# Copies of h, a power and the dense sums taken earlier, weight halves spread over ScalarE's waits, in a one-core attention and mixture-of-experts kernel

## The chip, the cores and the metric

The kernel runs on one core of one Trainium2 chip. The metric is device microseconds of one execution. The core has TensorE (PE in the rows, its weight loads PEld), VectorE (DVE), ScalarE (ACT), GpSimd (POOL) and the queue of SyncE (SP), which issues the transfers.

## The reference

```python
x = x + tanh(g_xattn) * attention(layernorm(x), ctx, ...)   # 8 batches x 128 tokens x 512, 32 heads, 8 kv heads
h = layernorm(x)                                            # seen by the router as 4 batches of 256 tokens
ratio = mean(|h[vision:]|) / (mean(|h[:vision]|) + 1e-8)    # one number for each batch
scores = softmax(concat(h, ratio) @ gate_w + gate_b)        # 3 experts
top_val, top_idx = top_k(scores, 2); top_val /= sum(top_val) + 1e-8
# an expert is chosen for each slot from the FIRST token: j = top_idx[:, 0, i]
pre = h @ w1[e] + b1[e]; act = (tanh, gelu, silu)[e](pre); out_e = act @ w2[e] + b2[e]
x = x + tanh(g_ffn) * (top_val[0] * out_of_slot_0 + top_val[1] * out_of_slot_1)
```

All arithmetic is float32. In the kernel a product of two float32 matrices is three products of rounded halves (hi x hi, lo x hi, hi x lo).

## The kernel before

The order of the work on each engine is written out by hand. Engines meet only in semaphores, and each engine takes its own instructions strictly in the order of the code.

The attention goes through 64 units (8 groups of heads x 8 batches) in a software pipeline, and ends in a drain. During and after the drain the second layer begins. Its steps, for batch b:

- `norm_row(1, b)` (ACT) writes the normalised row of h into `rows`. It needs the mean and the deviation: `h_stats(b)` (DVE), `h_pow(b)` (POOL, L1239), `h_neg_mean(b)` (DVE, L1467).
- `h_transpose(b)` (PE, L509) turns it into PSUM. From b = 4 on it waits for `h_lo_(b - 2)`, which frees the bank.
- `h_hi_(b)` (ACT, L1038) copies the rounded half into `xT_hi`, `h_lo_(b)` (DVE, L1280) the rest into `xT_lo`.
- `sum_abs(b)` (ACT, L1033) sums |h| for the ratio.

Six dense tiles follow on PE, `dense(l)` (L288, 12 matmuls each, into two PSUM banks in turn), for batches 0 and 1 and each expert. `dense_z(l)` (DVE, L1481) adds the bias and frees the bank, `dense_act(l)` (ACT, L1045) applies the function. Between them stand `gate_products` (PE, L711) with `gate_copy` (ACT, L1026), `ratio_sums` (PE, L775), and the two parts of `router` (PE, L786), which stand behind the first and the second of four chunks of `dense(4)`. `router(hf)` waits for `gate_copy(hf)` and for `tok0` (DVE, L1595). Ahead of `tok0` DVE makes the ratio in small steps, each waiting for the one before it (`settle()`): two scalings, a reciprocal, then a product (L1562), a product with the gate's row, and a sum. After `router` DVE forms softmax, comparisons and the picks (`picks_ok`); ACT gives the exponential in between.

The remaining items have a first tile only for the experts that were picked: `pair_first(j)` (PE, L288) waits for the picks, and for `dense_z(4)` and `dense_z(5)` where j is 4 and 5, since they free its bank. `pair_select(j)` (DVE, L1651) picks one of two results, `pair_transpose(j)` (PE, L509) turns it and waits for `pair_select(j)` and `pair_lo_(j - 1)`, `pair_hi_` (ACT, L1060) and `pair_lo_` (DVE, L1280) split it, `second_tile(j)` (PE, L288) multiplies by w2. `ranked_weights` and `weight_sums` (DVE) make the two weights in more small steps.

The weights of the second layer come in 20 pieces of 128x512, here numbered 0 to 19 (`W_D + n`): SP loads a piece into one of four buffers `wraw` once POOL is done with the piece four earlier; `w_expert_hi(n)` (ACT, L842) writes its rounded half; `w_expert_lo(n)` (POOL, L1168) subtracts and writes the rest. Both inputs of the POOL instruction lie in SBUF. Pieces 0 to 7 are needed by the dense tiles, the others are w2 and are needed by the `second_tile`s.

Of the kernel before, what the change touches and what calls it, by code (L numbers as in the profile page):

```python
# [78 lines left out]
W_D = W_A + KVH * W_PER  # L79
# [10 lines left out]
def build(nc, x, ctx_in, pos, mask, g_xattn, g_ffn, Wq, Wk, Wv, Wo, gate_w, gate_b, w1, b1, w2, b2,  # L90
          rope_rows, k_scratch, v_scratch, out):
    with ExitStack() as stack:
# [121 lines left out]
        def pair_at(j):  # L214
            return split[:, (2, 0)[j % 2], :, :]
# [5 lines left out]
        def both(j):  # L221

            slot, b = ITEMS[j]
            if j < CHOSEN:
                return [dense_at[e][b] for e in SLOT_EXPERTS[slot]]
            return [[rows[:, NROW - 1, :], unread], [roped[:, :], rot[:, 0, :]]][j % 2]

        def turn_of(j):

            return (1, 0) if ITEMS[j][0] == 1 and j % 2 == 1 else (0, 1)  # L230
# [92 lines left out]
        def tile_a(m):  # L323

            keys = TILE_ORDER[m] == "K"
            n = TILE_ORDER[:m].count(TILE_ORDER[m])
            return keys, n // B, n % B, n
# [26 lines left out]
        def h_bank(hb):  # L354

            return qbank[hb] if hb < 2 else (sbank, tbank)[hb % 2]
# [36 lines left out]
        def expert_target(n):  # L393
            at = EXPERT_BLOCK[(n - W_C) // EC]
            return [block_of(at, s) for s in range(2)], (n - W_C) % EC
# [442 lines left out]
        def _(act):  # L838
            def w_split_hi(n, k, dst):

                act.wait_ge(w_in[k], (n // NW + 1) * 16)
                act.activation(dst, wraw[:, k, :], ACT.Copy).then_inc(w_hi, 1)  # L842

            def norm_row(which, b):

                if which == 0:
                    act.wait_ge(ln_nmr, 1)
                    if b < NROW:
                        act.wait_ge(c_lo, PIECES - NROW + b + 1)
                    else:  # L850
                        act.wait_ge(row_t, b - NROW + 1)
                else:
                    act.wait_ge(h_nmr, b + 1)
                    if b >= NROW:
                        act.wait_ge(h_t, b - NROW + 1)
                    else:
                        act.wait_ge(row_t, B)
                act.activation(rows[:, b % NROW, :], xacc[:, b, :], ACT.Identity, bias=nmr[:, which, b:b + 1],
                               scale=rstd[:, which, b:b + 1]).then_inc((ln_row, h_row)[which], 1)
# [150 lines left out]
            def w_expert_hi(n):  # L1010
                if n == W_C + EC:
                    act.wait_ge(q_proj, UNITS)
                if n == W_C + 2 * EC:
                    act.wait_ge(s_done, UNITS - BH)
                if n == W_C + 3 * EC:
                    act.wait_ge(y_done, UNITS - B)
                if n == W_C + 4 * EC:
                    act.wait_ge(y_done, UNITS)
                if n == W_C + 5 * EC:
                    act.wait_ge(s_done, UNITS)  # L1020
                buf, k = expert_target(n)
                w_split_hi(n, n % NW, buf[0][:, k, :])

            def gate_copy(hf):
                act.wait_ge(gate_mm, hf + 1)
                act.activation(gate_rows[hf], gate_bank[hf], ACT.Copy).then_inc(gate_in, 1)  # L1026

            def sum_abs(hb):

                if hb >= 1:  # L1030
                    act.wait_ge(h_abs, hb)
                act.wait_ge(h_row, hb + 1)
                act.activation(unread, rows[:, hb % NROW, :], ACT.Abs, accum_out=absum[:, hb:hb + 1]  # L1033
                               ).then_inc(h_abs, 1)

            def h_hi_(hb):
                act.wait_ge(h_t, hb + 1)
                act.activation(xT[0][:, hb, :, :].rearrange("p c t -> p (c t)"), h_bank(hb)[:, :], ACT.Copy  # L1038
                               ).then_inc(h_hi, 1)

            def dense_act(l):

                b, e = DENSE[l]
                act.wait_ge(d_z, l + 1)
                act.activation(dense_at[e][b], dense_at[e][b], (ACT.Tanh, ACT.Gelu, ACT.Silu)[e]).then_inc(d_fn, 1)  # L1045

            def pair_act(j):

                for n, which in enumerate(turn_of(j)):
                    e = SLOT_EXPERTS[ITEMS[j][0]][which]  # L1050
                    act.wait_ge(f_z, 2 * (j - CHOSEN) + n + 1)
                    act.activation(both(j)[which], both(j)[which], (ACT.Tanh, ACT.Gelu, ACT.Silu)[e]).then_inc(f_fn, 1)

            def pair_hi_(j):
                act.wait_ge(f_t, j + 1)
                if j >= 2:
                    act.wait_ge(f2, j - 1)
                else:
                    act.wait_ge(y_done, UNITS)
                act.activation(pair_at(j)[:, 0, :], tbank[:, :], ACT.Copy).then_inc(pair_hi, 1)  # L1060
# [36 lines left out]
            norm_row(1, 5)  # L1097
            norm_row(1, 6)
            w_expert_hi(W_D + 9)
            sum_abs(4)  # L1100
            sum_abs(5)
            dense_act(0)
            dense_act(1)
            w_expert_hi(W_D + 10)
            h_hi_(4)
            h_hi_(5)
            norm_row(1, 7)
            h_hi_(6)
            sum_abs(6)
            sum_abs(7)  # L1110
            h_hi_(7)
            gate_copy(0)
            w_expert_hi(W_D + 11)
            gate_copy(1)
            w_expert_hi(W_D + 12)
            act.wait_ge(score_exp_in, 1)
            act.activation(exps, logit, ACT.Exp).then_inc(score_exp, 1)
            dense_act(2)
            dense_act(3)
            for k in range(13, 17):  # L1120
                w_expert_hi(W_D + k)
            dense_act(4)
            dense_act(5)
            w_expert_hi(W_D + 17)
            pair_hi_(0)
            w_expert_hi(W_D + 18)
            pair_act(4)
            w_expert_hi(W_D + 19)
            pair_hi_(1)
            pair_act(5)  # L1130
            pair_hi_(2)
            pair_hi_(3)
# [8 lines left out]
        def _(pool):  # L1141
# [24 lines left out]
            def w_split_lo(n, buf, c):  # L1166
                pool.wait_ge(w_hi, n + 1)
                pool.tensor_tensor(buf[1][:, c, :], wraw[:, n % NW, :], buf[0][:, c, :].bitcast(F32), ALU.subtract  # L1168
                                   ).then_inc(w_lo, 1)

            def w_expert_lo(n):
                w_split_lo(n, *expert_target(n))
# [9 lines left out]
            for m in range(TILES_A):  # L1182
                keys, half, k, n = tile_a(m)
# [52 lines left out]
            def h_pow(hb):  # L1236

                pool.wait_ge(h_var, hb + 1)
                pool.tensor_tensor(rstd[:, 1, hb:hb + 1], rstd[:, 1, hb:hb + 1], mhalf[:, 0:1], ALU.pow  # L1239
                                   ).then_inc(h_rstd, 1)  # L1240
# [27 lines left out]
            w_expert_lo(W_D + 8)  # L1268
            h_pow(6)
            w_expert_lo(W_D + 9)  # L1270
            w_expert_lo(W_D + 10)
            h_pow(7)
            for n in range(W_D + 11, W_END):
                w_expert_lo(n)

# [2 lines left out]
        def _(dve):  # L1278
            def subtract_hi(dst, src, hi, done):
                dve.tensor_tensor(dst, src, hi.bitcast(F32), ALU.subtract).then_inc(done, 1)  # L1280
# [58 lines left out]
            for m in range(TILES_A):  # L1339
                keys, half, k, n = tile_a(m)  # L1340
# [129 lines left out]
            def dense_z(l):  # L1470

                b, e = DENSE[l]
                dve.wait_ge(d_proj, l + 1)
                if l == 0:
                    dve.wait_ge(b1_in, 16 * NX)
                    dve.wait_ge(q_roped, UNITS)
                if e == 1:
                    dve.wait_ge(s_part, UNITS)
                if e == 2:
                    dve.wait_ge(p_t, UNITS)  # L1480
                dve.tensor_tensor(dense_at[e][b], qbank[l % 2][:, :], b1row[e], ALU.add).then_inc(d_z, 1)  # L1481
# [163 lines left out]
            def pair_select(j):  # L1645
                slot, b = ITEMS[j]
                if j < CHOSEN:
                    dve.wait_ge(d_fn, DENSE.index((b, (1, 2)[slot])) + 1)
                else:
                    dve.wait_ge(f_fn, 2 * (j - CHOSEN) + 2)  # L1650
                dve.copy_predicated(both(j)[0], masks[:, slot, b:b + 1].to_broadcast([P, 512]), both(j)[1]  # L1651
                                    ).then_inc(f_sel, 1)

            def pair_lo_(j):
                dve.wait_ge(pair_hi, j + 1)
                subtract_hi(pair_at(j)[:, 1, :], tbank[:, :], pair_at(j)[:, 0, :], pair_lo)
# [62 lines left out]
            def add_slot(j):  # L1719
# [4 lines left out]
                if slot == 0 and b >= NDENSE:  # L1724
# [3 lines left out]
                                         scalar=weight[:, slot, b:b + 1], in1=xacc[:, b, :], op0=ALU.mult, op1=ALU.add  # L1728
                                         ).then_inc(f_acc, 1)

            pair_select(0)
            dense_z(4)
            pair_select(1)
            ranked_weights()
            dense_z(5)
            pair_select(2)
            pair_add(4)
            pair_lo_(0)
            pair_select(3)
            pair_add(5)  # L1740
            pair_lo_(1)
# [72 lines left out]
```

## Time and profile before

| | |
|---|---|
| time, median of 3 runs | 703.7 us (702.28 to 704.24) |
| profiled execution | 702.35 us, of it the span of the trace 700.6 us |
| PE busy | 690.4 us of 700.6 |
| DVE, ACT, POOL busy | 558.7, 360.9, 401.4 us |

Busy time sums over the whole program; the change touches only the stretch from about 591 to 623 us of the span. In a row of the timeline the first number is the start in us from the span's start, the second the time until the end; rows overlap where instructions are pipelined. A bracket at the end of a row gives the idle time ahead of it and the instruction that ended it.

### The profile page before, as it was taken

Reading aid. Unit: us, or ns where it says so; the run is one execution under the profiler, and the core shown is the slowest. Engines: PE = TensorE matmul, PEld = TensorE weight load, DVE = VectorE, ACT = ScalarE, POOL = GpSimd, SP = SyncE. Lnnn points to the kernel's source line nnn. Section 1 sums busy time; section 2 is a strip of 40 time slices with the busy share of each in tenths; the row PEclk is TensorE's granted clock in tenths of the full one; section 3 lists DMA queues with packets and bytes.
Section 4 is the critical chain, followed back from the end, with each engine's and each line's share of the span. In section 5 each row is a group of like instructions: output and inputs, shape, how many; then the busy total and the mean of one; then the engine's idle time right before and its main releaser. Section 6 shows DMA issues by size and latency. Waiting matters only on the chain.

```text
span 700.6 us, 11568 instructions
## 1 busy us (share of the span) xinstructions
PE 690.4 (99%) x3479; PEld 578.4 (83%) x3479; DVE 558.7 (80%) x951; ACT 360.9 (52%) x961; POOL 401.4 (57%) x345
## 2 busy tenths in 40 slices
PE   8999999999999999999999999999999999999998
PEld 6888887888888888888888888888888887778886
DVE  5788776888887887887887887887887997587785
ACT  5625624545545545545545545555555688563522
POOL 5688855666666666666666666666566655240000
PEclk9999999999999999999999999999999999999999
DMA  8897564322222232131222222222232432130001
GB/s 265 316 334 288 195 198 148 107 75 75 62 90 63 60 92 60 60 90 60 62 77 74 62 88 60 64 86 60 69 82 61 135 90 78 47 91 31 1 31 60
DMA packets 65071, 70.84 MB, mean 101 GB/s; under 512 B 7680, under 2 KB 41472, under 8 KB 65024
## 3 DMA queue, kind: packets, MB, share of 16 engines
q1 hardware_dynamic: 64496, 68.98, 31.6%
q0 software_dynamic: 384, 1.05, 0.4%
q8 instruction: 19, 0.31, 0.2%
q10 hardware_dynamic: 144, 0.26, 0.1%
q14 instruction: 28, 0.23, 0.1%
HBM read 51.40 MB, written 18.87 MB: 100 GB/s over the span
## 4 chain that ended last, share of the span: by engine, by line
PE 85%; DVE 5%; ACT 3%; issue 2%; DMA 2%; POOL 1%; SPq 1%; DVEq 0%; ACTq 0%; POOLq 0%
PE q L298 29%; PE y L288 28%; PE o L665 6%; PE s L647 5%; PE q L288 5%; PE pt L509 4%; PE s L649 2%; PE pt L288 2%; PE o L288 2%; PE s L288 1%; PE s L509 1%; DVE big L1280 1%; DVE split L1280 1%; DMA rows<-ctx_t 1%; ACT prob L981 1%
## 5 line engine op out<-in xcount | busy, mean ns | idle before, releaser
L288 PE MATMUL y<-big,split 128*128 128x512 f32 (+1 forms) x864 | 209.3, 391 | 0.2
L288 PEld LDWEIGHTS y<-big,split 128*128 128x128 f32 x864 | 161.1, 188 | 33.8 <-DVE split L1280 0.6
L298 PE MATMUL q<-xT_hi,big 128*128 128x512 f32 x512 | 175.0, 403 | 0.0
L1218 POOL TENSOR_TENSOR roped<-rot 128x512 f32<-128x512 f32 x58 | 75.1, 1295 | 101.6 <-DVE rot L1306 101.6
L967 ACT ACTIVATE big<-roped 128x512 fp32r<-128x512 f32 x63 | 39.9, 633 | 141.9 <-POOL roped L1218 136.5
L298 PEld LDWEIGHTS q<-xT_hi,big 128*128 128x128 f32 x512 | 96.2, 188 | 19.2
L981 ACT ACTIVATE prob<-scores,nmax 128x128 f32<-128x128 f32 x256 | 99.9, 392 | 20.5 <-DVE nmax L1438 20.5
L1232 POOL TENSOR_TENSOR prob<-prob,prec 128x512 f32<-128x512 f32 x64 | 66.6, 1041 | 60.9 <-DVE prec L1443 60.9
L298 PE MATMUL q<-xT_lo,big 128*128 128x512 f32 x256 | 99.6, 389 | 0.0
L1221 POOL TENSOR_TENSOR big<-roped,big 128x512 fp32r<-128x512 f32 x63 | 81.5, 1293 | 13.4 <-ACT big L967 13.4
L1210 POOL TENSOR_TENSOR big<-wraw,big 128x512 fp32r<-128x512 f32 x64 | 83.1, 1299 | 0.0
L1443 DVE RECIPROCAL prec<-psums 128x4 f32<-128x4 f32 x64 | 11.4, 178 | 66.1 <-ACT prob L981 65.9
L647 PE MATMUL s<-kv,big 128*128 128x256 f32 x256 | 62.6, 322 | 0.3 <-POOL big L1221 0.3
L950 ACT ACTIVATE split<-o 128x512 fp32r<-128x512 f32 x57 | 34.0, 597 | 54.2 <-PE o L665 54.2
L1302 DVE TENSOR_TENSOR rot<-q,rope 128x512 f32<-128x512 f32 x72 | 49.1, 683 | 11.0 <-PE q L298 8.7
L1168 POOL TENSOR_TENSOR big<-wraw,big 128x512 fp32r<-128x512 f32 x32 | 41.0, 1292 | 27.9 <-ACT big L842 27.9
L649 PE MATMUL s<-kv,big 128*128 128x128 f32 x256 | 57.0, 223 | 0.0
L298 PEld LDWEIGHTS q<-xT_lo,big 128*128 128x128 f32 x256 | 48.4, 189 | 8.7
L665 PE MATMUL o<-split,kv 128*128 128x512 f32 x192 | 54.4, 391 | 0.6 <-DVE split L1280 0.6
L647 PEld LDWEIGHTS s<-kv,big 128*128 128x128 f32 x256 | 48.2, 188 | 3.5 <-POOL big L1221 1.0
L1447 DVE SCALAR_TENSOR_TENSOR xacc<-y,gates,xacc 128x512 f32<-128x512 f32 x64 | 47.9, 749 | 3.7
L649 PEld LDWEIGHTS s<-kv,big 128*128 128x128 f32 x256 | 48.8, 191 | 2.4
(200 smaller groups left out, 1273.1 us busy)
## 6 DMA issues: line engine op xcount, KB each, us to landing
wraw<-in_L_xattn_Wq SPq DMA_DIRECT2D x32, 256.0 KB
wraw<-in_L_xattn_Wo SPq DMA_DIRECT2D x32, 256.0 KB
kv<-k_scratch SPq DMA_DIRECT2D x64, 128.0 KB, 2.5
kv<-v_scratch SPq DMA_DIRECT2D x64, 128.0 KB, 2.9
v_scratch<-split SPq DMA_DIRECT2D x12, 512.0 KB, 3.9
wraw<-in_L_ffn_w SPq DMA_DIRECT2D x24, 256.0 KB
k_scratch<-split SPq DMA_DIRECT2D x10, 512.0 KB, 3.5
k_scratch<-kv SPq DMA_DIRECT2D x6, 512.0 KB, 3.8
```

The costliest lines, as they stand in the source:

```text
L288: mm = pe.matmul(bank_[:, :], stationary(s, c), moving(m, c), start=(c == 0 and n == 0), stop=(c == EC - 1 and n == 2))
L298: mm = pe.matmul(bank_[:, :].rearrange("p (b t) -> p b t", b=BH), weights[s][:, c, h * P:(h + 1) * P], source[m][:, half * BH:(half + 1) * ...
L647: pe.matmul(sbanks[:, 2 * h * P:(2 * h + 2) * P], q[0], kv[:, bs % NKV, 0:2, :].rearrange("p m k -> p (m k)"), start=True, stop=False)
L649: mm = pe.matmul(sbanks[:, 2 * h * P:(2 * h + 1) * P], q[1], kv[:, bs % NKV, 0, :], start=False, stop=True)
L665: mm = pe.matmul(obank[:, :], kv[:, bs % NKV, 2 + s, :], split[:, 1, m, :], start=(n == 0), stop=(n == 2))
L981: a = act.activation(prob[:, 0, h * P:(h + 1) * P], scores[:, h * P:(h + 1) * P], ACT.Exp, bias=nmax[:, turn, h:h + 1], accum_out=psums[:, ...
L1210: pool.tensor_tensor(buf[1][:, b % EC, :], wraw[:, b % NW, :], buf[0][:, b % EC, :].bitcast(F32), ALU.subtract).then_inc(w_lo, 1)
L1218: pool.tensor_tensor(roped[:, :], rot[:, 0, :], rot[:, 1, :], ALU.add).then_inc(q_roped, 1)
L1221: pool.tensor_tensor(q_split(1, bq // BH, bq % HG), roped[:, :], q_split(0, bq // BH, bq % HG).bitcast(F32), ALU.subtract).then_inc(q_lo, 1)
L1232: pool.tensor_tensor(heads(prob[:, 1, :]), heads(prob[:, 0, :]), prec[:, turn, :].unsqueeze(2).to_broadcast([P, HG, P]), ALU.mult).then_in ...
L1302: dve.tensor_tensor(to[:, 0, :], bank_[:, :], table(0, 0, D), ALU.mult)
L1447: dve.scalar_tensor_tensor(out=xacc[:, b3, :], in0=ybank[b3 % 2][:, :], scalar=gates[:, 0:1], in1=xacc[:, b3, :], op0=ALU.mult, op1=ALU.ad ...
```

## The change

```diff
--- before.py
+++ after.py
@@ -1097,36 +1097,38 @@
             norm_row(1, 5)
             norm_row(1, 6)
             w_expert_hi(W_D + 9)
+            h_hi_(4)
+            h_hi_(5)
             sum_abs(4)
+            dense_act(0)
+            norm_row(1, 7)
             sum_abs(5)
-            dense_act(0)
+            h_hi_(6)
             dense_act(1)
             w_expert_hi(W_D + 10)
-            h_hi_(4)
-            h_hi_(5)
-            norm_row(1, 7)
-            h_hi_(6)
             sum_abs(6)
+            h_hi_(7)
             sum_abs(7)
-            h_hi_(7)
             gate_copy(0)
             w_expert_hi(W_D + 11)
+            w_expert_hi(W_D + 12)
+            w_expert_hi(W_D + 13)
             gate_copy(1)
-            w_expert_hi(W_D + 12)
+            w_expert_hi(W_D + 14)
+            w_expert_hi(W_D + 15)
             act.wait_ge(score_exp_in, 1)
             act.activation(exps, logit, ACT.Exp).then_inc(score_exp, 1)
             dense_act(2)
             dense_act(3)
-            for k in range(13, 17):
-                w_expert_hi(W_D + k)
             dense_act(4)
+            w_expert_hi(W_D + 16)
             dense_act(5)
             w_expert_hi(W_D + 17)
             pair_hi_(0)
             w_expert_hi(W_D + 18)
             pair_act(4)
+            pair_hi_(1)
             w_expert_hi(W_D + 19)
-            pair_hi_(1)
             pair_act(5)
             pair_hi_(2)
             pair_hi_(3)
@@ -1268,8 +1270,8 @@
             w_expert_lo(W_D + 8)
             h_pow(6)
             w_expert_lo(W_D + 9)
+            h_pow(7)
             w_expert_lo(W_D + 10)
-            h_pow(7)
             for n in range(W_D + 11, W_END):
                 w_expert_lo(n)
 
@@ -1728,14 +1730,14 @@
                                          scalar=weight[:, slot, b:b + 1], in1=xacc[:, b, :], op0=ALU.mult, op1=ALU.add
                                          ).then_inc(f_acc, 1)
 
+            dense_z(4)
             pair_select(0)
-            dense_z(4)
+            dense_z(5)
             pair_select(1)
             ranked_weights()
-            dense_z(5)
-            pair_select(2)
             pair_add(4)
             pair_lo_(0)
+            pair_select(2)
             pair_select(3)
             pair_add(5)
             pair_lo_(1)
```

The instructions are the same but for where they stand. PE's and SP's orders do not change. The number of table loads on ACT is the same.

On ACT, just after the first two norm rows of the diff's first lines (L842 there is `w_expert_hi(9)`), before; L1033 is `sum_abs`, L1045 `dense_act`, L842 `w_expert_hi`, L1038 `h_hi_`, L858 `norm_row`, L1026 `gate_copy`, L1117 the exponential:

```order
 L842 ACTIVATE big<-wraw 128x512
-L1033 ACTIVATE rope,absum<-rows 128x512 x2
-L1045 ACTIVATE rot<-rot 128x512 x2
-L842 ACTIVATE big<-wraw 128x512
 L1038 ACTIVATE xT_hi<-s 128x512 x2
-L858 ACTIVATE rows<-xacc,nmr,rstd 128x512
+L1033 ACTIVATE rope,absum<-rows 128x512
+L1045 ACTIVATE rot<-rot 128x512
+L858 ACTIVATE rows<-xacc,nmr,rstd 128x512
+L1033 ACTIVATE rope,absum<-rows 128x512
```

`h_hi_(4)` and `h_hi_(5)` now follow piece 9 at once; two sums, two dense functions and piece 10 stood ahead of them.

On ACT again, somewhat later, at `gate_copy`:

```order
-L842 ACTIVATE big<-wraw 128x512
+L842 ACTIVATE big<-wraw 128x512 x3
 L1026 ACTIVATE rope<-o 8x512
-L842 ACTIVATE big<-wraw 128x512
-L1117 ACTIVATE scores<-scores 128x48
+L842 ACTIVATE big<-wraw 128x512 x2
+L1120 ACTIVATE scores<-scores 128x48
```

Pieces 11 to 15 now stand ahead of the exponential; pieces 11 and 12 did before, and 13 to 16 stood behind it and two dense functions.

On DVE, just behind the picks (the last row of L1627, L1629 in the changed file), before:

```order
L1627 CAST s<-scores 128x16
L1651 COPY_PREDICATED rot<-s,limit 128x512
L1481 TENSOR_TENSOR prob<-q0,rope 128x512
L1651 COPY_PREDICATED rot<-s,limit 128x512
L1562 TENSOR_TENSOR scores<-scores 128x8 x5
L1481 TENSOR_TENSOR prob<-q1,rope 128x512
L1651 COPY_PREDICATED prob<-s,limit 128x512
```

and of the change:

```order
L1629 CAST s<-scores 128x16
L1483 TENSOR_TENSOR prob<-q0,rope 128x512
L1653 COPY_PREDICATED rot<-s,limit 128x512
L1483 TENSOR_TENSOR prob<-q1,rope 128x512
L1653 COPY_PREDICATED rot<-s,limit 128x512
L1564 TENSOR_TENSOR scores<-scores 128x8 x5
L1644 TENSOR_TENSOR rows<-q0,rope 128x512
```

Both dense sums now stand ahead of the five small steps of `ranked_weights`, the first of them also ahead of a selection.

## Rows read from the trace of the kernel before

**Rows 1.** The page's line of busy time, and TensorE's granted clock in 40 slices

```profile
PE 690.4 (99%) x3479; PEld 578.4 (83%) x3479; DVE 558.7 (80%) x951; ACT 360.9 (52%) x961; POOL 401.4 (57%) x345
...
PEclk9999999999999999999999999999999999999999
```

**Rows 2.** The chain that ended last, one round late in the program (start, us, piece)

```profile
632.15 2.72 PE q L288 x12
634.87 0.44 PE s L509 x4
635.31 2.77 PE y L288 x12
```

**Rows 3.** Timeline of PE from 594 to 623 us

```profile
594.17 0.39 PE L288 MATMUL q<-big,xT_lo 128*128 128x512 f32 x1
595.50 0.63 PE L509 MATMUL s<-ident,rows 128*128 128x128 f32 x4 [0.94 <-DVE xT_lo L1280]
...
604.02 1.05 PE L786 MATMUL s<-fold,roped 8*128 8x4 f32 x8
...
611.11 0.39 PE L288 MATMUL q<-big,xT_lo 128*128 128x512 f32 x1
611.87 0.73 PE L288 MATMUL q<-big,xT_hi 128*128 x2 [0.37 <-DVE prob L1481]
...
615.98 0.72 PE L288 MATMUL q<-big,xT_hi 128*128 x2 [0.66 <-DVE prob L1481]
...
619.16 3.02 PE L288 MATMUL y<-big,split 128*128 x12
622.36 0.63 PE L509 MATMUL s<-ident,prob 128*128 128x128 f32 x4 [0.18 <-DVE split L1280]
622.75 3.00 PE L288 MATMUL y<-big,split 128*128 x12
```

**Rows 4.** Timeline of ACT from 590 to 604 us

```profile
590.60 0.61 ACT L842 ACTIVATE big<-wraw 128x512 fp32r<-128x512 f32 x1
...
594.05 1.06 ACT L1038 ACTIVATE xT_hi<-s 128x512 fp32r<-128x512 f32 x2
...
598.17 0.63 ACT L1033 ACTIVATE rope<-rows 128x512 f32<-128x512 f32 x1
...
598.80 0.58 ACT L1038 ACTIVATE xT_hi<-s 128x512 fp32r<-128x512 f32 x1
599.28 0.57 ACT L1026 ACTIVATE roped<-pt 8x512 f32<-8x512 f32 x1
599.76 0.61 ACT L842 ACTIVATE big<-wraw 128x512 fp32r<-128x512 f32 x1
603.44 0.59 ACT L1026 ACTIVATE rope<-o 8x512 f32<-8x512 f32 x1 [3.07 <-PE o L711]
```

**Rows 5.** Timeline of POOL from 600 to 617 us

```profile
600.45 1.28 POOL L1168 TENSOR_TENSOR big<-wraw,big 128x512 fp32r<-128x512 f32 x1 [4.45 <-ACT big L842]
604.62 1.27 POOL L1168 TENSOR_TENSOR big<-wraw,big 128x512 fp32r<-128x512 f32 x1 [2.89 <-ACT big L842]
611.26 5.05 POOL L1168 TENSOR_TENSOR big<-wraw,big 128x512 fp32r<-128x512 f32 x4 [5.37 <-ACT big L842]
```

**Rows 6.** Timeline of DVE from 602 to 612 us

```profile
602.33 0.17 DVE L1562 TENSOR_TENSOR scores<-scores 128x8 f32<-128x8 f32 x1
...
607.23 0.20 DVE L1562 TENSOR_TENSOR scores<-scores,s 128x48 f32<-128x48 f32 x1 [3.02 <-PE s L789]
...
611.05 0.68 DVE L1481 TENSOR_TENSOR prob<-q,rope 128x512 f32<-128x512 f32 x1
```

**Rows 7.** The chain that ended last, from 612 to 615 us

```profile
612.69 1.24 DVE scores L1562 x2
613.96 1.16 DVE scores L1562
```

**Rows 8.** Waits of PE over the whole span (us in total, times, longest)

```profile
PE o L562 <- POOL xT_hi L1142: 1.4, 1, 1.4
```

**Rows 9.** Windows around two loads (busy by engine, clock, DMA share, GB/s)

```profile
601.70:602.70 1.00, 1.00 (x6) 0.36 (x5) 0.90 (x6) 0.00 (x0) 0.03 (x1) 1.00 0.00 0
602.70:603.90 1.20, 1.20 (x7) 0.65 (x4) 0.45 (x4) 0.46 (x1) 0.00 (x0) 1.00 0.80 218
603.90:605.00 1.10, 1.10 (x9) 0.96 (x8) 0.16 (x1) 0.64 (x2) 0.38 (x1) 1.00 0.00 0
```

## The prediction, made before the changed kernel was run

> **What bounds the kernel now.** I read the busy times first: PE is busy for 690.4 of 700.6 us [rows 1]. Nothing gives time back here unless PE waits less. The chain that ended last then shows that from about 623 us to the end PE runs without a gap, in rounds of a first tile (2.72 us), a transposition (0.44) and a second tile (2.77) [rows 2]. The change cannot shorten that; it can only move its start. So the timeline of PE is left, between the drain and the first second tile, and it has four gaps [rows 3]:
>
> - 594.56 to 595.50: `h_transpose(6)` waits for `h_lo_(4)`. A matmul follows the one before it after 2.72 / 12 = 0.23 us, so it could have started at 594.17 + 0.23 = 594.40. The gap is worth 1.10 us.
> - Ahead of 611.87: `pair_first(4)` waits for `dense_z(4)`. It could have started at 611.11 + 0.23 = 611.34: 0.53 us.
> - Ahead of 615.98: `pair_first(5)` waits for `dense_z(5)`. From 611.87 to 615.98 are 4.11 us, and the same tile and transposition without a wait take 619.16 - 615.98 = 3.18: 0.93 us.
> - Ahead of 622.36: the third transposition waits for `pair_lo_(1)`. From 619.16 to 622.75 are 3.59 us instead of 3.18: 0.41 us.
>
> Together 2.97 us. That is the most that this change can win, and it is 0.4% of the time.
>
> **The copies of h and the last power.** `h_hi_(4)` and `h_hi_(5)` now follow piece 9 (590.60) instead of starting at 594.05 [rows 4]. The transposition they need ends near 591.5, so `h_hi_(4)` ends near 592.1. DVE is in `h_stats(7)` until about 592.8 and ends `h_lo_(4)` near 593.5, ahead of 594.40. The last power stands ahead of piece 10 on POOL, so `norm_row(1, 7)` comes near 593.7 and ends by 594.5, and PE wants it at 596.7. Two sums and a dense function are now behind the copies, but `sum_abs(7)` still ends near 598.5, and `ratio_sums` wants it near 599.9. Nobody waits for piece 10, which moves from 593.5 to about 596. The gap of 1.10 us goes, and PE reaches `router(0)` at 604.02 - 1.10 = 602.9 (a warm transposition saves 0.03 more).
>
> **The weight halves.** On ACT they fill idle time, 3.07 us ahead of `gate_copy(1)` [rows 4], and cost nothing there. But each brings a POOL instruction of 1.27 us behind it [rows 5], which reads two inputs from SBUF, and this is where I see a price. At 612.27 DVE starts the five small steps of `ranked_weights`, while POOL does four halves in a row from 611.26, one ending every 1.27 us. DVE's steps, of 0.17 us elsewhere [rows 6], take 1.24 and 1.16 us [rows 7], and they end at 613.9 and 615.1, just behind POOL's third and fourth start. A DVE instruction with two SBUF inputs is held until POOL's current instruction ends; DVE then gets one step in, and POOL's next one holds the step after it. The Trainium skill's page "SBUF — State Buffer" ("SBUF: two separate sides") states a lock of this kind between a DVE operation with two SBUF inputs and a GpSimd operation that reads SBUF, exclusive for the whole instruction; the trace agrees, with its 1.24 us.
>
> Before, the steps that make the ratio ran free: POOL's half of piece 11 ended at 601.73, the first such step began at 602.33 [rows 5, 6]. Now, in the times of before:
>
> - ACT: `sum_abs(7)` starts at 597.8, right behind `h_hi_(7)`. `gate_copy(0)` follows at 598.45 (0.63 us later, as 598.17 to 598.80), piece 11 at 598.93, pieces 12 and 13 each 0.52 us on.
> - POOL starts the half of a piece 0.69 us behind ACT's start (599.76 to 600.45): 599.62, 600.88 and 602.15, the last ending at 603.42.
> - ACT does `gate_copy(1)` at 603.44 - 1.13 = 602.31, piece 14 at 602.79, piece 15 at 603.31. POOL takes them at 603.49 and 604.75, ending at 606.0. The load of piece 15 starts when piece 11 is done (600.9) and has 2.4 us; the load that started at 601.73 moved its bytes between 602.7 and 603.9 and was over by then, 2.2 us after [rows 9].
> - DVE's first step with two SBUF inputs is ready at 602.33 - 1.13 = 601.20, and ends with POOL's second half at 602.2. The product with the gate's row ends with the third at 603.5. The sum is ready at 603.53, and POOL starts again at 603.49: held until 604.8. `tok0` is then held by piece 15's half until 606.1.
>
> So `router(0)` starts near 606.25 in place of 604.02. This is 2.2 us later than before, and PE stands still for 3.3 us. If instead the sum slips in ahead of POOL at 603.5, which 0.05 us decide, one hold falls away and `router(0)` starts near 605.1, 1.1 us later than before. Bounds of this term: no hold at all, -1.13 us; four holds, +2.2 us. I take four, since the tie leans that way.
>
> **The dense sums.** From `router` on all of DVE's picks shift alike: softmax starts at 607.23 + 2.2, and POOL is then idle until piece 16. `dense_z(4)` is now first behind the picks, at 610.3 + 2.2 = 612.5 to 613.2, and PE wants it at 611.34 + 2.2 = 613.5. It was at 611.05 [rows 6]. `dense_z(5)` ends near 614.6, and is wanted at 616.7. Both gaps go: -0.53 and -0.93 us. The selection that now stands behind is wanted at 616.4 and done at 614.0. PE's read of the pick from SBUF has 1 us, as the picks are ready at 612.4.
>
> **The ranking** starts at 615.2 on DVE. ACT finishes pieces 16 and 17 at 615.2 and 616.3, so POOL is busy from 615.3 to 617.85, and the steps are held twice, until 617.9. `pair_add(4)` starts then, 1.4 us after its tile; `pair_lo_(0)` ends at 619.85, just as the second tile wants it at 619.9. The two selections and `pair_add(5)` follow, and `pair_lo_(1)` ends near 623.0. The third transposition would want 622.75, so it starts near 623.15: about 0.4 us of wait, as before. The fourth gap stays (bounds 0 and -0.41).
>
> **The sum**, against the profiled 702.35 us: +2.2 - 0.53 - 0.93 + 0 = +0.8 us, so 703.1 us; on the median of 703.7 us it is 704.5, and I give 704.4 since the tie pulls down a little. A difference under about 0.3% (2.1 us) a measurement of this kernel can hardly tell.
>
> **The rivals.**
>
> - One hold fewer: +1.1 - 0.53 - 0.93, with or without 0.41 more, so -0.4 to -0.8 us: 703.1. For it speaks the tie of 0.05 us; it leaves the sign open but not the verdict. Chance 0.28, beside 0.40 for four holds.
> - The halves and the small steps miss each other, because POOL runs earlier than I have it, or the ratio's steps are not held. Then all gaps go: -2.97 us, 700.7. For it: every such step but those at 612 us was short in the trace. Against it: POOL has a row of three halves, 3.8 us long, and the first step falls 0.3 us inside the second. Chance 0.17. It decides if fewer than two holds occur: -2.97 + 1.26 is still -1.7, which counts as no change.
> - Slower, by TensorE's clock. The granted clock was full in all 40 slices [rows 1], and the longest wait of PE in the whole span was 1.4 us [rows 8]. A stand of 3.3 us is something that this trace does not show. If the clock falls from 2.4 to 1.2 GHz behind it, a tile of 2.72 us takes 5.44. With +0.8 from the sum, half a tile at the low level (+1.36) reaches the bound of 2.1 us, and one whole tile gives +3.5: 707.2. Against it: PE does 1 us of matmuls shortly ahead of it and after it without a gap. Chance 0.10.
> - The change does nothing at `h_transpose(6)`, because `h_lo_(4)` is late by another wait, while the holds stay: 1.1 us more than my sum, 705.6. `h_lo_(4)` has 0.9 us of room, so 0.05.
>
> **How the numbers follow.** Faster 0.17, from the second rival. Slower 0.12: the clock with 0.10, and 0.02 from the last one. The rest, 0.71, is within the bound. The range takes in the gain without holds nearly whole, 701.0, and above it the sum with one more wait, 705.9; of the clock's case most stays out.
>
> **What would show it.** In the profile of the changed kernel: no idle time at `h_transpose(6)`; POOL with three or five halves in a row from about 599.6; L1564 steps of more than 1 us near 601 to 604, and a long step at L1597; a wait of PE of 2 to 3.3 us ahead of `router(0)`, released by `tok0`; no idle time ahead of `pair_first(4)` and `pair_first(5)`; two long steps of `ranked_weights`. If the ratio's steps are short, I am wrong by up to 3.7 us. If the clock shows under 1.00 from 606 to 612 us, the third rival holds.

## The result and the profile after

The changed kernel takes 706.95 us (median of 14 runs, 704.84 to 709.19), the kernel before 702.76 us (14 runs, 701.65 to 704.24). The ratio is 1.0058, 95% interval 1.0045 to 1.0070; the medians differ by 4.2 us. The prediction was 704.4 us, 0.7 us above the 703.7 us then known for the kernel before, within a range that ended at 705.9.

The page's busy times and the granted clock of the changed kernel, for [rows 1]:

```profile
PE 692.8 (98%) x3479; PEld 580.5 (82%) x3479; DVE 562.1 (80%) x951; ACT 361.1 (51%) x961; POOL 401.8 (57%) x345
...
PEclk9999999999999999999999999999999999899999
```

One digit has changed: in one slice of 17.6 us the clock of TensorE was not full. PE is busy for 2.4 us more, although it does the same instructions.

The waits of PE over the whole span, for [rows 8] (us in total, times, longest):

```profile
PE s L786 <- DVE scores L1597: 3.2, 1, 3.2
...
PE o L562 <- POOL xT_hi L1144: 1.4, 1, 1.4
```

A wait of 3.2 us that was not there stands first: `router(0)` waits for `tok0`. The timeline of PE, for [rows 3]:

```profile
595.81 0.60 PE L509 MATMUL s<-ident,rows 128*128 128x128 f32 x4
...
607.57 1.02 PE L786 MATMUL s<-fold,roped 8*128 8x4 f32 x8 [3.20 <-DVE scores L1597]
608.52 1.22 PE L288 MATMUL q<-big,xT_hi 128*128 128x512 f32 x2
...
617.93 0.61 PE L288 MATMUL q<-big,xT_hi 128*128 x2
...
621.01 0.71 PE L288 MATMUL q<-big,xT_hi 128*128 x2
...
624.22 3.00 PE L288 MATMUL y<-big,split 128*128 x12
627.06 0.60 PE L509 MATMUL s<-ident,prob 128*128 128x128 f32 x4
627.42 2.79 PE L288 MATMUL y<-big,split 128*128 x11
```

To compare times of this trace with those of before, 1.41 us are taken off: it is that much later already at the pair of transpositions ahead of the change (592.20 for 590.79), from waits in the first 100 us that differ from run to run. All four gaps of before are gone; none of these rows but `router(0)` has a bracket. `router(0)` starts at 607.57 - 1.41 = 606.16, 2.14 us later than before (predicted 606.25). The second tile at 627.42 starts 627.42 - 1.41 - 622.75 = 3.26 us later. Of the 2.14, the three later gaps give back 0.53 + 0.93 + 0.41 = 1.87, which leaves 0.27. So 3.0 us (3.26 - 0.27) are lost between `router(0)` and the rounds, with PE never idle. Windows over that stretch show where (busy by engine, then the granted clock):

```profile
607.00:608.00 1.00, 0.43 (x4) 0.47 (x5) 0.50 (x2) 0.00 (x0) 0.39 (x1) 1.00 0.81 168
608.00:609.00 1.00, 1.00 (x7) 0.98 (x7) 0.00 (x0) 0.00 (x0) 0.00 (x0) 0.73 0.83 258
609.00:610.00 1.00, 1.00 (x3) 0.34 (x2) 0.00 (x0) 0.00 (x0) 0.00 (x0) 0.50 0.78 219
...
613.00:614.00 1.00, 1.00 (x4) 0.81 (x3) 0.62 (x4) 0.80 (x2) 0.00 (x0) 0.50 0.14 53
614.00:616.00 2.00, 2.00 (x8) 1.59 (x7) 1.77 (x13) 1.97 (x4) 0.00 (x0) 0.68 0.01 2
```

From about 608.5 to 615.3 the clock is at 0.50, the 1.2 GHz level, for 6.8 us. This is why PE's busy time grew: two matmuls at 608.52 take 1.22 us instead of 0.73.

DVE in the changed kernel, for [rows 6, 7], and POOL beside it, for [rows 5]:

```profile
602.59 0.98 DVE L1564 TENSOR_TENSOR scores<-scores 128x8 f32<-128x8 f32 x1
603.61 2.61 DVE L1564 TENSOR_TENSOR scores<-scores,gwm 128x24 f32<-128x24 f32 x3
606.25 1.17 DVE L1597 TENSOR_TENSOR scores<-roped,fold 8x16 f32<-8x16 f32 x1
...
618.13 0.69 DVE L1483 TENSOR_TENSOR prob<-q,rope 128x512 f32<-128x512 f32 x1 [1.15 <-PE q L288]
...
619.38 2.02 DVE L1564 TENSOR_TENSOR scores<-scores 128x8 f32<-128x8 f32 x5
```

```profile
601.01 6.38 POOL L1170 TENSOR_TENSOR big<-wraw,big 128x512 fp32r<-128x512 f32 x5 [1.54 <-ACT big L842]
618.43 1.30 POOL L1170 TENSOR_TENSOR big<-wraw,big 128x512 fp32r<-128x512 f32 x1 [11.04 <-ACT big L842]
620.09 1.29 POOL L1170 TENSOR_TENSOR big<-wraw,big 128x512 fp32r<-128x512 f32 x1 [0.35 <-ACT big L842]
```

POOL does five halves in one row, from 601.01 to 607.39. Four dependent steps of DVE fall into it (the row of three steps holds two long ones, each over 1.2 us), and each ends just behind a half.

### The profile page after: what moved, and what is told of

Its sections match the earlier page's. It is cut to its first block, busy times and chain, and to the rows that moved or that the text cites. A ratio compares the mean times of both kernels' runs of the same rounds, so it can differ in the third digit from the quotient of the medians.

```text
span 705.3 us, 11568 instructions
## 1 busy us (share of the span) xinstructions
PE 692.8 (98%) x3479; PEld 580.5 (82%) x3479; DVE 562.1 (80%) x951; ACT 361.1 (51%) x961; POOL 401.8 (57%) x345
## 3 DMA queue, kind: packets, MB, share of 16 engines
q0 software_dynamic: 384, 1.05, 0.5%
## 4 chain that ended last, share of the span: by engine, by line
PE 88%; DVE 5%; DMA 2%; ACT 1%; issue 1%; SPq 1%; POOL 1%; DVEq 0%; ACTq 0%; POOLq 0%
PE q L298 29%; PE y L288 28%; PE q L288 7%; PE o L665 6%; PE s L647 5%; PE pt L509 4%; PE s L649 2%; PE o L288 2%; PE pt L288 2%; PE s L509 1%; DMA rows<-ctx_t 1%; PE s L288 1%; ACT prob L981 1%; DVE split L1282 1%; DVE big L1282 1%
```

## The experiments

Each was timed against the kernel before, on the same chip. The clock is given for each execution; where it is named, it is the mean over the whole execution, so 0.997 stands for some 4 us at the low level and 0.992 for 11 us ((1 - 0.992) x 2 x 705). Two cautions go with such a mean. It counts low time in which PE has nothing left to do: in the profile of the changed kernel PE is done at 702.0 us, and the clock is low again from 704.0 us to the end of the span at 705.3. And in the three series that follow, the kernel before itself shows a mean under 1.00 in 29 of 79 executions (0.995 once, 0.997 or 0.998 otherwise), with a median of 702.9 us against 702.7 us in the other 50. Where those falls lie no profile shows. So a mean of 0.997 alone does not say that a fall cost time.

**The halves back (e1_halves_back).** The changed kernel, with pieces 12 to 19 at their places of before:

```diff
             w_expert_hi(W_D + 11)
-            w_expert_hi(W_D + 12)
-            w_expert_hi(W_D + 13)
             gate_copy(1)
-            w_expert_hi(W_D + 14)
-            w_expert_hi(W_D + 15)
+            w_expert_hi(W_D + 12)
...
             dense_act(3)
+            for k in range(13, 17):
+                w_expert_hi(W_D + k)
             dense_act(4)
...
```

> The changed kernel, but the weight halves of pieces 12 to 19 back at their places of before; the copies of h, the last power and the dense sums stay early. Theory (the halves' POOL work holds the ratio's small DVE steps, TensorE stands 3.2 us at router(0), and its clock falls behind that stand): no long DVE step ahead of router(0), no stand there, clock 1.00 throughout, and 2.5 to 2.9 us faster than the kernel before. Rival (the loss comes from the early copies or sums, or the clock falls for a reason of its own): still slower than before by 2 us or more.

Median 702.58 us, ratio 1.0009 (0.9992 to 1.0026). The cause is confirmed, the size is not: there is no long step ahead of `router(0)` and no stand there. But the ranking, now behind both dense sums, runs into POOL's halves at another place. The five steps of the ranking in the kernel before and in this one, then PE of this one:

```profile
612.27 2.83 DVE L1562 TENSOR_TENSOR scores<-scores 128x8 f32<-128x8 f32 x5
```

```profile
612.58 3.50 DVE L1562 TENSOR_TENSOR scores<-scores 128x8 f32<-128x8 f32 x5
```

```profile
618.15 0.63 PE L509 MATMUL s<-ident,rot 128*128 128x128 f32 x4 [0.89 <-DVE split L1280]
```

The ranking takes 3.50 us instead of 2.83, the first pair half comes late, and PE stands 0.89 us at the second pair transposition. In this profile the rounds still start 1.9 us earlier than before (with 0.85 us taken off, as above), and the clock is 1.00. Of the ten executions, those with clock 1.00 took 701.3 to 702.6 us, and three with 0.994 or 0.995 took 703.9, 704.7 and 706.7 (the other three, at 0.998 and 0.999, 702.5 twice and 704.7). The kernel before had 0.995 once in 79 executions and nothing below, so even a stand of this size seems to be followed by a fall of the clock at times; no profile caught one. The median of the other seven is 702.5 us, so these three do not explain why the 1.9 us of the profile are missing in the medians, and that stays open. With four pieces in a row behind the exponential, the early sums only move the stall to the second pair transposition.

**The halves alone (e2_halves_alone).** The kernel before with the opposite of that diff.

> The kernel before with the weight halves alone spread as in the change. Theory: the ratio's steps begin 1.1 us later than in the change, so they meet three of POOL's halves, TensorE stands about 2.0 us at router(0); 2 us slower than before if the clock keeps 1.00 through such a stand, about 5 us slower if it falls as behind the 3.2 us. Rival (the halves are harmless without the other two moves): within 0.5 us of before.

Median 705.8 us, ratio 1.0037 (1.0024 to 1.0051), 3.1 us slower. The chain shows three held steps (0.73, 1.24 and, for `tok0`, 1.34 us) and one free sum (0.19 us):

```profile
602.29 0.73 DVE scores L1564
...
603.05 1.24 DVE scores L1564
...
604.41 0.19 DVE scores L1564
604.62 1.34 DVE scores L1597 x2
605.97 0.05 issue
606.02 1.06 PE s L786 x8
```

PE waits 2.0 us at `router(0)`. The clock falls here too, for 6.8 us in the profile; over the ten executions it is 0.993 to 0.997. The theory holds with the clock's term; the sum of 5 us was too high. It left out that a slower PE takes up the three later waits of before: 2.0 us at `router(0)`, 3.0 through the clock, less 1.87, is the 3.2 us by which the rounds start later in the profile.

**One operand in PSUM (e3_psum_operands).** The full change, but with `ratio` and `part` in PSUM, and `tok0` read from the PSUM of the gate products:

```diff
-        part = scores[:, 11 * B:14 * B].rearrange("p (b e) -> p b e", e=NX)
+        ratio = sbank[:, 288:288 + B]
+        part = sbank[:, 320:320 + NX * B].rearrange("p (b e) -> p b e", e=NX)
...
-                                  gate_rows[hf].rearrange("p (b t) -> p b t", t=P)[:, :, 0:1].to_broadcast([8, BH, 4]),
+                                  gate_bank[hf].rearrange("p (b t) -> p b t", t=P)[:, :, 0:1].to_broadcast([8, BH, 4]),
```

> The changed kernel in its full order, but ratio and the product with the gate's row are kept in PSUM, and the first-token product reads the gate products from PSUM, so that each of the ratio's steps has only one input in SBUF. Theory (a DVE instruction is held by POOL when two of its inputs lie in SBUF): the steps take 0.2 us each beside POOL's halves, no stand at router(0), clock 1.00, 2.6 to 3.0 us faster than before. Rival (POOL holds any small DVE instruction, or DVE's write): steps of 1.2 us remain and the time is that of the change.

Median 700.23 us, ratio 0.9963 (0.9951 to 0.9974): 2.5 us faster than before and 6.7 us faster than the change. DVE and POOL:

```profile
601.12 0.17 DVE L1565 TENSOR_TENSOR s<-s,scores 128x8 f32<-128x8 f32 x1
601.33 0.19 DVE L1565 TENSOR_TENSOR s<-s,gwm 128x24 f32<-128x24 f32 x1
601.55 0.27 DVE L1565 TENSOR_TENSOR scores<-s,gwm 128x24 f32<-128x24 f32 x2
601.86 0.16 DVE L1598 TENSOR_TENSOR scores<-pt,fold 8x16 f32<-8x16 f32 x1
```

```profile
599.52 6.39 POOL L1171 TENSOR_TENSOR big<-wraw,big 128x512 fp32r<-128x512 f32 x5 [1.54 <-ACT big L843]
```

POOL does the same five halves in a row, and the same four steps run through them in 0.9 us, where they took 4.8. PE has no wait from 585 to 630 us, and the clock is 1.00 in the profile and in three other executions; it is 0.997 in the remaining three of the seven, about as often as in the kernel before. The rounds start 3.0 us earlier than before. This is the version that beats both kernels. The rival, that POOL holds any small instruction or DVE's write, falls: the third and fourth rows write to SBUF and are short.

**A stand made by other means (e4_late_6).** The kernel before, with reads that only take DVE's time:

```diff
+            for k in range(6):
+                dve.bn_stats(bn[:, 0, k % B, :], xacc[:, k % B, :])
             for hf in range(2):
                 dve.wait_ge(gate_in, hf + 1)
```

> The kernel before, with six extra BN_STATS reads of xacc by DVE (0.61 us each, their result unused) ahead of the first-token product; nothing else moves, and POOL does nothing new. Theory (a stand alone makes the clock fall): TensorE stands about 3.0 us at router(0), the clock falls to 0.50 for some 7 us soon after, and the kernel is about 6 us slower than before. Rival (the fall needs something else of the change): clock 1.00 and 3.0 us slower.

Median 707.52 us, ratio 1.0058 (1.0040 to 1.0076), 4.8 us slower for a stand of 2.8 us. The windows have the clock at the low level from about the end of the stand on:

```profile
605.00:607.00 2.00, 0.00 (x0) 0.00 (x0) 2.00 (x4) 0.00 (x0) 1.27 (x1) 1.00 0.00 0
607.00:609.00 2.00, 1.63 (x8) 1.66 (x8) 0.31 (x3) 0.00 (x0) 0.00 (x0) 0.51 0.47 143
...
617.00:619.00 2.00, 2.00 (x10) 1.66 (x9) 1.97 (x6) 1.98 (x5) 1.89 (x2) 0.93 0.00 0
```

No half was moved here. So the stand is enough for the fall; nothing else of the change is needed. The fall begins at 607.06 us, 0.3 us before the stand ends.

**The copies alone (e5_h_alone).** The kernel before with the first part of ACT's hunk, and with the last power early:

```diff
             w_expert_hi(W_D + 9)
+            h_hi_(4)
+            h_hi_(5)
             sum_abs(4)
...
             h_pow(6)
             w_expert_lo(W_D + 9)
+            h_pow(7)
             w_expert_lo(W_D + 10)
-            h_pow(7)
```

> The kernel before with the early copies of h and the early last power alone. Theory (each of the moves is a gain where the prediction had it, and only the halves cost): no wait at the seventh transposition of h, the waits of 0.37 and 0.66 us at the pair tiles stay, the ratio's steps are free since POOL's half of piece 11 ends at 600.9; 1.1 us faster. Rival (the early copies cost something too): not faster.

Median 702.0 us, ratio 0.9981 (0.9969 to 0.9994): 0.8 us faster, 1.1 expected. In the profile the wait at the seventh transposition is gone, and those of 0.36 and 0.67 us at the pair tiles stay.

**The sums alone (e6_sums_alone).** The kernel before with DVE's hunk alone:

```diff
-            pair_select(0)
             dense_z(4)
+            pair_select(0)
+            dense_z(5)
             pair_select(1)
             ranked_weights()
-            dense_z(5)
-            pair_select(2)
             pair_add(4)
             pair_lo_(0)
+            pair_select(2)
```

> The kernel before with the dense sums ahead of the selections and the ranking alone. Theory: the waits at the pair tiles go (-1.46 us), but the five steps of the ranking now start at 613.0 instead of 612.3 and are held by POOL's four halves until 616.3, so that the first pair half is late and TensorE stands about 0.95 us at the second pair transposition, as in the kernel with the halves back; with the later wait of 0.4 us gone too, about 0.9 us faster where the clock keeps 1.00. Rival (the steps pass POOL): 1.9 us faster.

Median 703.04 us, ratio 1.0005 (0.9987 to 1.0024). The waits at the pair tiles are gone, and PE stands 0.92 us at the second pair transposition, as expected. In the profile the rounds start 0.7 us earlier than before. Eight executions took 701.1 to 703.8 us; two, with clock 0.994 and 0.995, took 705.3 and 706.6. The median of the eight, 702.7 us, is no more than 0.2 us below that of before, so the expected 0.9 us is not shown; it lies just inside the interval.

**Shorter stands (e7_late_4, e8_late_3, e11_late_2).** The diff of e4 with four, three and two reads.

> The kernel before with four extra DVE reads ahead of the first-token product: by the 2.8 us with six, TensorE stands 2.8 - 2 x 0.61 = 1.6 us at router(0). Theory (the clock falls only behind a stand of about 2 us or more): clock 1.00, 1.6 us slower. Rival (any stand at this place, between tiles with little for TensorE, is enough): clock falls, 4 us slower.

> The same with three extra reads: a stand of 1.0 us. Theory: clock 1.00, 1.0 us slower. Rival: the clock falls here too, 3.5 us slower.

> The kernel before with two extra DVE reads ahead of the first-token product, which end at about 604.3, ahead of POOL's half of piece 12, so that nothing is held (with three reads the product fell behind the start of that half, and the stand was 1.96 us where 1.0 was expected). TensorE stands about 0.5 us at router(0). Theory (a short stand leaves the clock alone): clock 1.00, 0.5 us slower. Rival (any stand at this place is enough): the clock falls, 3 us slower.

Four reads: 706.01 us, ratio 1.0044 (1.0030 to 1.0059). Three: 705.68 us, ratio 1.0034 (1.0019 to 1.0049). In both PE stood 1.96 us, not the expected 1.6 and 1.0, and the clock fell. With three reads DVE and POOL show why:

```profile
603.15 1.88 DVE L1594 BATCH_NORM_STATS2 bn<-xacc 128x6 f32<-128x512 f32 x3
604.95 1.05 DVE L1597 TENSOR_TENSOR scores<-roped,fold 8x16 f32<-8x16 f32 x1
```

```profile
604.71 1.26 POOL L1168 TENSOR_TENSOR big<-wraw,big 128x512 fp32r<-128x512 f32 x1 [2.88 <-ACT big L842]
```

The late `tok0` missed POOL's start by 0.24 us and was held until its end. I had forgotten the very hold that I was testing. Neither run tells anything on stands of 1 us. With two reads `tok0` came ahead of POOL; PE stood 0.46 us, the clock kept 1.00 in six of ten executions and was 0.997 or 0.998 in the others, as in the kernel before: 703.49 us, ratio 1.0012 (1.0000 to 1.0024).

**PSUM without the moves (e9_psum_before).** The diff of e3 on the kernel before.

> The kernel before with ratio and the product with the gate's row in PSUM and the first-token product read from PSUM, and nothing else. Theory (in PSUM the steps are not faster by themselves, they only escape POOL's halves, and before none met one): within 0.5 us of before, so that the gain of the third run comes from the moves. Rival (the PSUM operands are a gain of their own): 1 us or more faster.

Median 703.01 us, ratio 1.0006 (0.9994 to 1.0018). The PSUM operands gain nothing by themselves.

**Two holds (e10_two_holds).** The diff of e3 on the changed kernel, without the line for `ratio`.

> The changed kernel with the product with the gate's row in PSUM and the first-token product read from PSUM, but ratio itself still in SBUF, so that two of the four steps that POOL held keep two SBUF inputs. Theory: holds only at the ratio's product and at the product with the gate's row, then free steps; TensorE stands about 1.1 us at router(0). That gives 1.1 - 2.97 = 1.9 us faster where the clock keeps 1.00, and about 1.5 us slower where it falls; with a stand between the 0.5 us and the 2.0 us seen so far I expect a fall in some executions. Rival (each hold costs its 1.27 us wherever it lies, and clock always falls): slower by 1.5 us in all.

Median 703.33 us, ratio 1.0009 (0.9998 to 1.0021). DVE has two long steps and then short ones, and PE stands 1.14 us:

```profile
601.96 0.99 DVE L1564 TENSOR_TENSOR scores<-scores 128x8 f32<-128x8 f32 x1
602.99 1.24 DVE L1564 TENSOR_TENSOR s<-scores,gwm 128x24 f32<-128x24 f32 x1
604.25 0.27 DVE L1564 TENSOR_TENSOR scores<-s,gwm 128x24 f32<-128x24 f32 x2
```

```profile
604.87 1.02 PE L786 MATMUL s<-fold,roped 8*128 8x4 f32 x8 [1.14 <-DVE scores L1597]
```

```profile
608.00:610.00 2.00, 2.00 (x6) 1.61 (x6) 1.47 (x8) 1.22 (x2) 0.00 (x0) 0.50 0.79 220
610.00:612.00 2.00, 2.00 (x8) 1.58 (x7) 1.81 (x12) 1.97 (x4) 0.00 (x0) 0.66 0.84 287
```

Here the clock is low for 3.4 us, and the fall begins 3.1 us after the stand has ended. None of the ten executions has 1.00; they have 0.994 to 0.997, where 16 of the 25 of the kernel before have 1.00. Against the 700.6 us that I had for a full clock (702.54 us for before, less 1.9), the median lies 2.7 us higher. In the profile the fall cost 1.5 us (the table below); the rest of the 2.7 is not explained.

## Why the prediction was wrong

**Right: the four gaps.** All four are gone; e5 shows the first one alone, and e3, in which nothing else is in the way and the clock is full, is worth 3.0 us in the profile and 2.5 us in the medians, where 2.97 was the most.

**Right: the holds.** The term "four holds, +2.2 us" measured +2.14; the stand was to be 3.3 us and is 3.20. Four steps are long in the trace, as listed. That two SBUF inputs are the condition was only argued from one place of the trace of before; e3 against the change shows it, and e9 shows that nothing else hides in that edit. The page "SBUF — State Buffer" of the Trainium skill ("SBUF: two separate sides") names the same condition, and the 0.17 us and 0.98 us of the same step with one and with two SBUF inputs agree with it.

**Wrong in size, harmless: the ranking.** I had it start at 615.2, be held twice, and kept the fourth gap of 0.41 us. In the changed kernel it starts at 619.38 - 1.41 = 617.97, since `dense_z(5)` ahead of it waits 1.15 us for a tile that PE does late, and the five steps take 2.02 us: piece 17 came 0.35 us after piece 16 was done and left DVE room between them. The gap went, but here the low clock may have helped. In e3, at full clock, the five steps take 1.71 us beside two halves in a row, and no wait of PE is left. So on the moves alone the sum would have been +0.27 us, not +0.8.

**Wrong: the clock.** The step that failed is that the sum put the clock at nothing behind a stand of 3.3 us. The runs showed a fall for 6.8 us that cost 3.0 us. I had it as the third rival, "Slower, by TensorE's clock", with the right mechanism and place, but with a chance of 0.10, and the range stopped short of it. That its 707.2 us is so near to the median of 706.95 is partly luck: it stood on 703.7 us for the kernel before, which 14 runs put at 702.76, on +0.8 us where the moves gave +0.27, and on one tile, 5.4 us, at the low level where there were 6.8. What I held against it, that PE works shortly ahead of the stand and without a gap behind it, did not keep the clock up. I read a full clock in 40 slices as support, but those slices could not speak on such a stand. Even the wait of 1.4 us that I named as the longest [rows 8] is the time ahead of PE's first matmul, at 1.39 us; once PE had begun, its longest wait was the 0.94 us at `h_transpose(6)`. The price in the profile, 3.0 us, is somewhat under half of the 6.8 us at the low level. Over the 14 executions the clock is 0.992 to 0.995, never 1.00. The six with 0.995 took 704.8 to 706.9 us, the seven with 0.992 or 0.993 took 706.6 to 709.2, so some were low for longer, and it cost more. Of the 4.2 us between the medians the profile accounts for 3.3; of the other 0.9, the longer falls can be a part, and how large a part is not shown.

By size, a stand of 0.46 us left no mark beyond those of the kernel before, and 0.9 us at another place was followed by 0.994 or 0.995 in some executions. For the longer stands the profiles give the price. It is what the second tile of the rounds starts later than before, less what `router(0)` does, plus the 1.87 us of the three later waits, which are gone in all of these (us):

| run | stand | clock low for | lost through the clock |
|---|---|---|---|
| e10 | 1.14 | 3.4 | 1.5 |
| e2 | 1.96 | 6.8 | 3.0 |
| e8 | 1.96 | 6.8 | 3.1 |
| e7 | 1.96 | 10.2 | 4.6 |
| e4 | 2.83 | 10.2 | 4.5 |
| the change | 3.20 | 6.8 | 3.0 |

The price goes with the time at the low level, 0.43 to 0.45 of it in each row, and not with the length of the stand: the same stand of 1.96 us cost 3.0 us in one profile and 4.6 in another. What decides how long the clock stays low is not settled by these runs.

## What to carry to other kernels

Idle time of ScalarE is not free to fill, if every instruction put there starts one on GpSimd: ask which small VectorE steps with two SBUF inputs will then run beside it. Here each dependent step cost up to a whole GpSimd instruction of 1.27 us, and an operand moved to PSUM freed it. Where a sum makes TensorE stand longer than it stands anywhere in the trace once it has begun, add the clock as a term of the sum and not as a remote case. And read such a sum on the profile: a gain of 1 or 2 us in one execution (e1, e6) can be missing in the medians.

## What the runs showed of the hardware

- A VectorE instruction that waits for GpSimd gets in when GpSimd's current instruction ends, even with GpSimd's next one ready: five halves in a row lasted 6.38 us with four steps let in between (the changed kernel), and 6.39 us with none held (e3).
- `BATCH_NORM_STATS2` reading 512 elements of SBUF ran at 0.61 us each beside GpSimd's half in e4, with no hold; a product of 8 x 16 elements with two SBUF inputs took 1.05 us in e8, held by the same kind of half.
- A fall of the clock came with stands of TensorE down to 1.14 us. It began between 0.3 us before the end of the stand (e4) and 3.1 us after it (e10), lasted 3.4, 6.8 or 10.2 us, and cost 1.5, 3.0 or about 4.5 us in the profiles, besides the stand.
